# A hybrid block in one kernel: the experts' second product as three fp32r products, with split gated values

## The reference

```python
x = x + attn_a(layernorm(x))
x = x + ffn(layernorm(x))
x = x + attn_b(layernorm(x))
x = x + ffn(layernorm(x))

def ffn(x):                      # 8 experts, the best 2 count, 16 numbers inside each
    logits = einsum('bth,eh->bte', x, router_w)
    weights = softmax(logits)
    gate = weights * topk_mask(weights, 2)
    h = einsum('bth,eih->beti', x, down_w)
    out = einsum('beti,ehi->beth', silu(h), up_w)
    return einsum('beth,bte->bth', out, gate)
```

## Time and profile before

| | us |
|---|---|
| median of three runs | 1275.09 (1273.79 to 1275.57) |
| the profiled execution | 1279.85 |
| its span | 1278.0 |
| TensorE busy with matmuls | 1143.4 (89 %) |
| VectorE busy | 821.7 (64 %) |
| GpSimd busy | 799.3 (63 %) |
| ScalarE busy | 613.1 (48 %) |
| TensorE's mean granted clock | 0.962 of full |
| `tail` in the trace | about 902 to 1278 |

### The profile page before, as it was taken

How to read it: one execution, slowest core, us unless ns; L and a number is a source line. 1 busy time by engine, 2 the same in 40 slices (tenths; PEclk the granted TensorE clock), 3 DMA queues, 4 the chain that set the end, 5 groups by cost and what they waited for, 6 DMA issues and landing times. The chain is left out here.

```text
span 1278.0 us, 20694 instructions
## 1 busy us (share of the span) xinstructions
PE 1143.4 (89%) x7552; PEld 627.5 (49%) x7552; DVE 821.7 (64%) x1423; ACT 613.1 (48%) x1000; POOL 799.3 (63%) x586
## 2 busy tenths in 40 slices
PE   6999967999689899898898898898899999999995
PEld 5888622343233343243343333332467777777552
DVE  6886275667366557647646655650497788876885
ACT  4444225656556666566576565566442222222221
POOL 2012159579979879779698797776126666666211
PEclk9999969999899999999999998998999999999997
DMA  8333340120230220221212022004422312222431
GB/s 271 97 121 107 102 101 26 51 67 26 68 90 26 67 67 31 61 67 59 69 56 67 18 62 80 1 1 149 150 84 74 122 68 66 67 75 75 165 108 42
DMA packets 69956, 99.16 MB, mean 78 GB/s; under 512 B 12384, under 2 KB 35808, under 8 KB 69856
## 3 DMA queue, kind: packets, MB, share of 16 engines
q1 hardware_dynamic: 61024, 74.77, 20.2%
q0 software_dynamic: 4224, 14.68, 3.0%
q10 hardware_dynamic: 4608, 8.39, 1.8%
HBM read 64.25 MB, written 33.55 MB: 77 GB/s over the span
## 5 line engine op out<-in xcount | busy, mean ns | idle before, releaser
L1090 DVE TENSOR_REDUCE nm<-score 128x1 f32<-128x640 f32 (+6 forms) x352 | 349.5, 1026 | 272.8 <-PE score L981 222.4
L1257 POOL TENSOR_TENSOR base<-base,plain 128x2048 f32<-128x2048 f32 (+2 forms) x78 | 301.0, 3860 | 16.1 <-ACT plain L1206 6.2
L1206 ACT ACTIVATE plain<-score 128x1024 f32<-128x1024 f32 (+3 forms) x288 | 207.2, 734 | 108.2 <-PE score L997 61.2
L992 PE MATMUL score<-q,k 98*128 98x512 bf16 (+7 forms) x768 | 195.0, 340 | 51.0 <-ACT plain L1206 20.4
L1206 ACT ACTIVATE base<-score 128x1024 f32<-128x1024 f32 x96 | 97.5, 1023 | 72.8 <-PE score L997 51.4
L992 PEld LDWEIGHTS score<-q,k 98*128 98x128 bf16 (+1 forms) x768 | 54.8, 99 | 154.6 <-DVE nm L1090 57.7
L1010 PE MATMUL acc<-plain,vg 128*32 128x512 f32 (+3 forms) x1152 | 114.7, 471 | 0.0
L976 PE MATMUL score<-k,q 48*128 48x512 bf16 (+3 forms) x512 | 70.3, 354 | 17.7 <-DVE nm L1090 17.5
L1594 PE MATMUL m_b<-m_winh,m_hTh 128*128 128x512 f32 x192 | 83.7, 436 | 1.4 <-DVE m_k L1864 1.4
L1594 PE MATMUL m_b<-m_winh,m_hTl 128*128 128x512 f32 x192 | 75.9, 395 | 0.0
L1594 PE MATMUL m_b<-m_winl,m_hTh 128*128 128x512 f32 x192 | 75.7, 394 | 0.0
(11 more groups left out here) (253 smaller groups left out, 2491.6 us busy)
## 6 DMA issues: line engine op xcount, KB each, us to landing
q<-piece_scratch SPq DMA_DIRECT2D x192, 64.0 KB, 2.7
k<-piece_scratch SPq DMA_DIRECT2D x192, 64.0 KB, 2.2
piece_scratch<-n_pieces SPq DMA_DIRECT2D x16, 384.0 KB, 3.0
piece_scratch<-pieces POOLq DMA_DIRECT2D x8, 768.0 KB, 4.0
n_x1in<-in_query SPq DMA_DIRECT2D x16, 256.0 KB, 3.7
v_scratch<-n_v ACTq DMA_DIRECT2D x16, 256.0 KB, 2.1
vg<-v_scratch SPq DMA_DIRECT2D x8, 512.0 KB, 4.7
att_scratch<-m_qT SPq DMA_DIRECT2D x8, 512.0 KB, 3.0
```

The source lines that it names most:

```text
L992: mm = nc.tensor.matmul(score[k % RING][:, x, t0:HALF], kst[n % SLOTS][c, first + x, j * P:(j + 1) * P], qst[n % SLOTS][c, first + x, h * ...
L1090: nc.vector.tensor_reduce(out, src, AX.X, ALU.max, negate=True).then_inc(s_max, 1)
L1206: nc.scalar.activation(tile_of(n, v)[:, first:first + 2, t0:HALF], score[k % RING][:, :, t0:HALF], ACT.Exp)\
L1257: nc.gpsimd.tensor_tensor(total, total, tile_of(n, v)[:, :, t0:HALF], ALU.add)\
```

## The change

The experts' second product becomes three fp32r products. The weights `up` are loaded to a place that `h2` uses later, and split once, by ScalarE (`uph`) and VectorE (`upl`), in round 1. The transposed gated values are split in every round: ScalarE rounds them to `gaTh`, VectorE subtracts (`gaTl`, new `dve_gaT`), near the start of its round and ahead of `rest_a` and `add_x`. In rounds 16 and on, TensorE transposes the gated values ahead of `pe_turn` and of the last quarter of the product. A table of `lnbb` moves into `h2` as well. Its core:

```diff
+    def dve_gaT(self, dve, t, bank):
+        dve.wait_ge(self.s_gaT, t + 1)
+        self.nc.vector.tensor_tensor(self.gaTl[:, t % 2], bank[:, 0:P], self.gaTh[:, t % 2].bitcast(F32), ALU.subtract)\
+            .then_inc(self.s_gaTl, 1)
+
...
-        self.nc.scalar.copy(self.gaT[:, t % 2], bank[:, 0:P]).then_inc(self.s_gaT, 1)
+        self.nc.scalar.copy(self.gaTh[:, t % 2], bank[:, 0:P]).then_inc(self.s_gaT, 1)
...
     def pe_up(self, pe, t, bank):
-        pe.wait_ge(self.s_gaT, t + 1)
-        self.nc.tensor.matmul(bank[:], self.gaT[:, t % 2], self.w["up"][:], start=True, stop=True)\
-            .then_inc(self.s_u, 1)
+        pe.wait_ge(self.s_gaTl, t + 1)
+        high, rest = self.gaTh[:, t % 2], self.gaTl[:, t % 2]
+        for n, (x, y) in enumerate(((high, self.w["uph"]), (rest, self.w["uph"]), (high, self.w["upl"]))):
+            mm = self.nc.tensor.matmul(bank[:], x, y[:], start=(n == 0), stop=(n == 2))
+        mm.then_inc(self.s_u, 1)
...
                 if NT <= s < 2 * NT:
                     last_product(s, range(KC - 1))
+                if NT - 2 <= s - 2:
+                    ex.pe_turn_ga(pe, s - 2, bu)
                 if 0 <= s - 1 < 2 * NT:
                     ex.pe_turn(pe, s - 1, t0)
                 if NT <= s < 2 * NT:
                     last_product(s, range(KC - 1, KC)).then_inc(s_w, 1)
-                if 0 <= s - 2 < 2 * NT:
+                if 0 <= s - 2 < NT - 2:
                     ex.pe_turn_ga(pe, s - 2, bu)
...
+                if s == 2:
+                    pe.wait_ge(s_upl, 1)
...
+                if s >= 2:
+                    ex.dve_gaT(dve, s - 2, bu)
                 if WHOLE < s + 1 < NT:
                     rest_a(s + 1)
                 if s < 2 * NT:
...
                 if s + 1 == WHOLE:
+                    dve.wait_ge(s_uph, 1)
+                    vec.tensor_tensor(w["upl"][:], up, w["uph"][:].bitcast(F32), ALU.subtract).then_inc(s_upl, 1)
                     rest_a(WHOLE)
...
                 if s + 1 == WHOLE:
+                    act.wait_ge(s_const, 16 * NCONST)
+                    nc.scalar.copy(w["uph"][:], up).then_inc(s_uph, 1)
                     round_a(WHOLE)
```

More of the change, by code:

```diff
@@ L265, in build @@
                 **small, ident=ident, tri=sb("tri", [P, NX, NX]), win=win, wo=wo,
-                down=sb("down", [P, KC, NX * IX + NX]), up=sb("up", [P, E]), bout=sb("bout", [P, E]),
+                down=sb("down", [P, KC, NX * IX + NX]), uph=sb("uph", [P, E], F32R), upl=sb("upl", [P, E], F32R), bout=sb("bout", [P, E]),
                 wab=place[:, 0:B * KC * E].rearrange("p (b c e) -> p b c e", b=B, c=KC),
@@ L1340, in __init__ @@
         self.rank, self.gate = sb("rank", [P, NX]), sb("gate", [P, NX])
-        self.ga, self.gaT = sb("ga", [P, 2, NH]), sb("gaT", [P, 2, P])
+        self.ga, self.gaTh, self.gaTl = sb("ga", [P, 2, NH]), sb("gaTh", [P, 2, P], F32R), sb("gaTl", [P, 2, P], F32R)
         self.half = sb("half", [P, 2])
@@ L1346, in __init__ @@
         self.s_h, self.s_top, self.s_e, self.s_gate = sem("s_h"), sem("s_top"), sem("s_e"), sem("s_gate")
+        self.s_gaTl = sem("s_gaTl")
         self.s_ga, self.s_tg, self.s_gaT, self.s_u, self.s_x2 = (sem(n) for n in ("s_ga", "s_tg", "s_gaT", "s_u",
@@ L1476, in tail @@
         lnw, lnb = w["lnw"], w["lnb"]
-        lnbb = sb("lnbb", [P, KC, P])
         bin_ = sb("bin", [P, 3 * E])
@@ L1488, in tail @@
         h2 = sb("h2", [P, 2, E])
+        up, lnbb = h2[:, 0], h2[:, 1].rearrange("p (c t) -> p c t", c=KC)
         hTh, hTl = sb("hTh", [P, 2, E], F32R), sb("hTl", [P, 2, E], F32R)
@@ L1506, in tail @@
         s_aTh, s_aTl, s_hTl, s_wh, s_wl = (sem(n) for n in ("aTh", "aTl", "hTl", "wh", "wl"))
-        s_wout, s_rope = sem("wout_in"), sem("rope")
+        s_wout, s_rope, s_uph, s_upl = (sem(n) for n in ("wout_in", "rope", "uph", "upl"))
         s_w, s_st2, s_rr, s_r, s_grow, s_h2 = (sem(n) for n in ("w", "st2", "rr", "r", "grow", "h2"))
@@ L1560, in _ @@
                       (w["tri"][:], a["c_tri"].rearrange("p (e f) -> p e f", e=NX)),
-                      (w["up"][:], a["up_w"].rearrange("e i h -> (e i) h"))]
+                      (up, a["up_w"].rearrange("e i h -> (e i) h"))]
             later = [(bin_[:], a["b_in"].rearrange("(o n) -> o n", o=1).broadcast_to([P, 3 * E])),
@@ L1733, in _ @@
             vec = nc.vector
-            vec.tensor_copy(lnbb[:], lnb[:].rearrange("p (c o) -> p c o", o=1).broadcast_to([P, KC, P]))\
+            vec.tensor_copy(lnbb, lnb[:].rearrange("p (c o) -> p c o", o=1).broadcast_to([P, KC, P]))\
                 .then_inc(s_fold2, 1)
```

## The result

| | before | changed |
|---|---|---|
| median | 1275.27 us (1273.79 to 1275.57, four runs) | 1297.95 us (1296.77 to 1299.29, four runs) |
| the profiled execution, its span | 1279.85, 1278.0 us | 1298.01, 1296.2 us |
| TensorE busy | 1143.4 us | 1136.1 us |
| VectorE busy | 821.7 us | 828.7 us |
| mean granted clock | 0.962 | 0.964 |

The changed kernel takes 1.0177 times as long (95 % interval 1.0163 to 1.0191), 22.7 us more. The forecast was 1299.6, in a range of 1290 to 1312.

What follows compares the result with a forecast made beforehand. In late rounds TensorE and VectorE, nearly equal, run side by side; the change closes their loop every round. +20.5 at full clock and +4 for the clock, +24.5 on the median 1275.09, gave 1299.6 us, range 1290 to 1312.

Steps and rivals of the forecast that it cites:

- the sum at full clock: Whole tail without any fall of the clock: 0.7 + 1.2 + 2.0 + 15.3 + 1.3 = +20.5 us.
- start, to `add_x` 19: Tail to round 19: weights' split and two subtractions 1.1, rounds 16 to 19 return 0.6, later `add_x` 0.25; +0.7 us.
- round 19 to 20: To round 20: `add_x` starts 1.87 us behind the gated values instead of 0.70, +1.2 us.
- rounds 20 to 22: Two rounds of 7.64 and 7.81 us, the latter with VectorE's columns' work, against 13.49: +2.0 us.
- rounds 22 to 31: Nine late rounds of 7.64 us, 68.8 against 53.45: +15.3 us.
- behind round 31: Last transposition of a tile waits for gated values at half clock speed: +1.3 us, without it 0.
- the clock in the late rounds: TensorE rests about 1.8 us each late round; a fall costing 0.8 in every second of eleven: +4 us, ends 0 and 16.
- The loop: Late rounds: VectorE's next round waits for gated values' transposition and copy, 1.87 us (product branch 1.78); round 7.64 us.
- The subtraction's price: VectorE's new 128-column subtraction per round: 0.21 us to the next instruction's start, not its 0.29.
- The product's saving: Three fp32r products instead of the f32 pair save TensorE 0.16 us a round, 5.1 us over 32 rounds.
- the rival of the other side: TensorE is the bound and the change pays: 32 x 0.16 would give 1270 us; chance 0.03.
- The rival "the clock holds": No fall of the clock in the late rounds: 1275.1 + 20.5 = 1295.6 us; chance 0.25.

Runs made afterwards that it cites:

- the move alone: Kernel before, with only TensorE's early transposition of the gated values from round 16 on, f32 product, no split: 1296.04 us, ratio 1.0154.
- the subtraction alone: Changed kernel with the gated values' transposition back behind the product's last quarter, the subtraction still ahead of `add_x`: 1287.77 us, ratio 1.0082.
- the order mended: Changed kernel with the transposition in its old place and VectorE's subtraction behind `add_x` in rounds 16 to 31: 1277.7 us, ratio 0.9998.
- the longer rests: Changed kernel with one, then three unused 512-column VectorE additions ahead of the gate in rounds 21 to 31: 1309.44 and 1326.82 us.
- one addition: Changed kernel with one unused 512-column VectorE addition ahead of the gate in rounds 21 to 31: 1309.44 us, one run.
- three additions: Changed kernel with three unused 512-column VectorE additions ahead of the gate in rounds 21 to 31: 1326.82 us, one run.

## Why the prediction was right, step by step

The direction, the mechanism and the place were right, and the time lies 1.6 us under the forecast. That it is so near is in part luck: 4 us for a fall of the clock that did not come make up for 0.7 us that the sum at full clock missed, and for 1.7 by which the medians differ from the ledger (1.5) and the median of before had moved (0.2). The parts, with "later by" from the ledger:

| step | predicted | measured |
|---|---|---|
| start, to `add_x` 19 | +0.7 | +1.4 |
| round 19 to 20 | +1.2 | +1.14 |
| rounds 20 to 22 | +2.0 | +1.95 |
| rounds 22 to 31 | +15.3 | +15.57 |
| behind round 31 | +1.3 | +1.1 |
| sum at full clock | +20.5 | +21.2 |
| the clock in the late rounds | +4 | 0 |

**The loop.** The chain 0.06, 0.17, 0.64, 0.47, 0.28, 0.04, 0.21 (1.87) came out as 0.06, 0.16, 0.64, 0.48, 0.38 for ScalarE's copy with its release, and 0.20: 1.92. With 5.75 instead of 5.77 that is 7.67 for 7.64. Each of the two branches has a run of its own: 1.77 through the product (the move alone) for my 1.78, 1.00 through the subtraction where ScalarE is free. They run side by side, so they don't add: the move alone costs 1.60 us a round, the subtraction alone 0.81, both 1.73.

**The subtraction's price.** 0.20 to 0.21 us from its start to that of the next instruction, not its 0.29 (1241.68 to 1241.88). The run with the subtraction behind `add_x` confirms it in another place (1237.20 to 1237.40). The rule of the Trainium skill that I weighed against it (VectorE: DVE Perf Modes, The DRAIN you can't avoid) would charge 0.29; no trace here shows that. The same section of the Trainium skill goes on to say that a next instruction which isn't held starts earlier, and the rows agree (0.20 us).

**The product's saving.** 0.15 us a product (1.87 against 1.72) for the 0.16 from the rows. By the four passes of the Trainium skill, FP8 and Floating Point Precision, TensorE Precision Notes, it would be 0.22, an estimate, and no run shows that. The saving brought nothing, against the rival of the other side: in the late rounds of the changed kernel neither engine is full, and with the order mended VectorE is.

**The start** cost twice what I had put on it. The weights' split and two subtractions were to cost 1.1 by round 4; it is 0.92 (0.77 when round 2 starts, then 0.18 once). But from round 11 to 16 another 0.6 comes on, where I had put nothing. Of this 0.25 us is the split's: the step from `add_x` 11 to 12 takes 14.85 to 14.97 us in all nine traces with the split and 14.60 to 14.65 in the three without. What makes it isn't settled; in that round VectorE's addition to `k` starts 6.55 us behind `add_x` in the changed kernel and 6.28 in the one before. The rest of the 0.6 is no more than two executions of the kernel before differ by (0.9 at round 15). Between rounds 16 and 19 I had 0.6 given back and 0.25 lost again by the later copy, 0.35 in all; 0.2 came. With the move and without the late subtractions it is 0.2 as well, with the subtractions and without the move 0.4, with neither 0.5. So the small return comes more with the move than with the subtraction, though the differences are tenths of a microsecond from one trace each.

**The clock** is the step that failed: "I take 0.8 in every second of eleven rounds, +4". I had the rest right (1.8, measured 1.75 to 1.78 in eight of nine), and carried over the one near row, 1.95 us in the attention part, which a fall followed. None did here. Two figures on the way were off besides: a granted clock of 0.73 in the microsecond behind 864.00 puts the fall about 0.5 us behind the rest and not 0.7, and 0.8 in every second of eleven rounds is 4.4. The price for a fall was right in size (0.8, measured 0.7 to 1.2 with the longer rests); whether there is one was wrong. With this term at 0 the forecast would have been 1295.6, 2.4 us below the result, of which 0.7 is the sum's and 1.7 the medians' as above. The rival "the clock holds" described what happened better than my forecast did.

**The signs that I had named.** `add_x` 7.6 apart: 7.67. Subtraction waiting 1.6 for ScalarE: 1.71. Transposition waiting 1.8: 1.77. Rounds 5 to 13 at 14.6: 14.61 to 14.69, but for 14.88 from `add_x` 11 to 12. `add_x` 8 to 8.5 apart at a low clock: not seen.

## What to carry to other kernels

Where two engines of nearly the same length take turns in handing work to each other, find the instruction that ends an engine's round and ask how many instructions stand between it and the start of that engine's next round. As long as its consumer comes late in the order, the two engines slide past each other; once anything ahead of the next round's first instruction needs it, each round pays the whole trip, here 1.9 us on top of 5.75. Cheaper arithmetic moves nothing then, and the busy shares, which fall on both engines at once, are the sign of it. Put a new small step behind the first instruction of a round instead of ahead of it; beside a round of 5.87 without it, the same subtraction cost 0.88 us a round in one place and 0.08 in the other.

## What the runs showed of the hardware

- Rests of TensorE of 1.75 to 1.88 us, nine in 65 us, were followed by no fall of the granted clock. With one addition six rests of 2.09 to 2.48 us in the same rounds all went with a fall, with three additions seven of 2.67 to 3.58 did and three of 2.14 to 2.19 did not. One of 1.95 us before, in the attention part, was followed by one too.
- A fall of the clock cost a round 0.7 to 1.2 us, less than the 1.47 us by which, as an estimate from the rows, the transpositions and the quarter product on the loop (0.17 + 1.30) would grow at half speed.
- Two independent instructions of VectorE, the first of 0.29 us, start 0.20 us apart, also when the first reads a bank of matmul results and writes fp32r (1241.68 to 1241.88).
- An f32 product of 512 columns costs 0.15 us more than three fp32r products in its place (1.87 against 1.72 us from the `down` product to the next round's).
